# Turning x by VectorE blocks and a trip through memory in the last stage, with the experts one piece of heads later

## The reference, cut to what matters

```python
x = x + attention(layernorm(x))     # 32 heads of 128, ends in y @ Wo.T  (512 <- 4096)
n = layernorm(x)
result = n @ W.T + b
q, k   = n @ Wq.T, n @ Wk.T          # 8 experts of 32 each
w      = softmax(sum(q * k, -1) / sqrt(32))      # one weight per expert
h      = n @ A.T                     # 8 experts of rank 16
x = x + result + einsum(w, h, Bm)
```

## Time and profile before

| | us |
|---|---|
| median of 3 runs | 1765.15 (1765.02 to 1765.41) |
| the profiled execution | 1765.26 |
| its span in the trace | 1763.4 |
| TensorE busy | 1738.6 (99%) |
| VectorE busy | 1271.4 (72%) |
| ScalarE busy | 715.1 (41%) |
| GpSimd busy | 851.6 (48%) |

### The profile page before, as it was taken

The page is one execution under the profiler, slowest core; times in us unless marked ns, Lnnn a source line. Parts: engine busy times, 40 slices in busy tenths (PEclk is TensorE's granted clock), DMA queues, the critical chain, the costliest instruction groups (busy, mean ns, idle before and its releaser), DMA issues. The chain is left out here.

```text
span 1763.4 us, 27984 instructions
## 1 busy us (share of the span) xinstructions
PE 1738.6 (99%) x8744; PEld 1468.0 (83%) x8744; DVE 1271.4 (72%) x2353; ACT 715.1 (41%) x2232; POOL 851.6 (48%) x862
## 2 busy tenths in 40 slices
PE   7999999999999999999999999999999999999998
PEld 6788888888888888888888888888778888888886
DVE  5327899998989989889999998998864333333332
ACT  3424444444455444544445444544652212121111
POOL 3126676667667666767666666766401101010101
PEclk9999999999999999999999999999999999999999
DMA  6235323433433333332433333333572323232321
GB/s 208 91 100 146 91 73 118 116 93 112 120 87 118 118 86 111 114 102 77 118 117 90 111 120 88 118 88 105 195 253 76 99 78 102 76 103 74 104 73 47
DMA packets 145985, 190.31 MB, mean 108 GB/s; under 512 B 9136, under 2 KB 79792, under 8 KB 145840
## 3 DMA queue, kind: packets, MB, share of 16 engines
q1 hardware_dynamic: 145840, 188.58, 35.6%
HBM read 141.89 MB, written 46.66 MB: 107 GB/s over the span
## 5 line engine op out<-in xcount | busy, mean ns | idle before, releaser
L117 POOL TENSOR_TENSOR q<-raw_wo_early 128x512 f32<-128x512 f32 x128 | 165.3, 1291 | 195.8 <-DVE raw_wo_early L109 195.6
L88 PE MATMUL p_proj<-shared,wq_hi 128*128 128x512 f32 x744 | 244.5, 389 | 0.0
L1135 ACT ACTIVATE square<-p_y 128x128 f32<-128x128 f32 x512 | 134.2, 277 | 220.1 <-PE p_y L849 218.7
L1877 POOL TENSOR_TENSOR var<-mv,eps 128x1 f32<-128x1 f32 x16 | 3.0, 190 | 402.6 <-DVE mv L1727 402.6
L849 PE MATMUL p_y<-v_tok,probs 128*128 128x128 f32 x1024 | 183.0, 276 | 0.0
L1007 DVE SCALAR_TENSOR_TENSOR z<-p_y,srstd,gate 128x128 f32<-128x128 f32 x512 | 143.7, 343 | 51.6 <-issue 34.5
L1110 ACT ACTIVATE probs<-g_row,stab 128x128 f32<-128x128 f32 x512 | 164.3, 407 | 24.2 <-POOL g_row L1244 24.1
L88 PE MATMUL p_kept<-wg_hi,shared 128*128 128x512 f32 x560 | 173.1, 390 | 0.0
L1258 POOL TENSOR_TENSOR xw_lo<-xw_raw,xw_hi 128x512 fp32r<-128x512 f32 x96 | 131.0, 1364 | 86.0 <-ACT xw_hi L1151 86.0
L88 PEld LDWEIGHTS p_proj<-shared,wq_hi 128*128 128x128 f32 x744 | 139.7, 188 | 30.4 <-DVE raw_wo_early L109 1.2
L1266 POOL TENSOR_TENSOR srstd<-svar,mhalf 128x4 f32<-128x4 f32 x128 | 157.7, 1232 | 10.0
(11 more groups left out here) (244 smaller groups left out, 4395.3 us busy)
## 6 DMA issues: line engine op xcount, KB each, us to landing
g_row<-g_scratch SPq DMA_DIRECT2D x128, 256.0 KB, 5.1
z_scratch<-z_st SPq DMA_DIRECT2D x256, 128.0 KB
w_raw<-z_scratch SPq DMA_DIRECT2D x62, 512.0 KB, 6.7
e_row<-e_scratch SPq DMA_DIRECT2D x96, 256.0 KB, 4.1
w_raw<-in_wq_t SPq DMA_DIRECT2D x16, 512.0 KB, 7.3
w_raw<-in_wg_t SPq DMA_DIRECT2D x16, 512.0 KB, 5.6
v_tok<-v_scratch SPq DMA_DIRECT2D x32, 256.0 KB, 2.9
v_scratch<-n_xin SPq DMA_DIRECT2D x20, 256.0 KB, 2.3
```

The costliest lines, as they stand in the source:

```text
L88: mm = pe.matmul(out, lhs[a], rhs[e], start=(i == 0 and j == 0), stop=(i == len(pairs) - 1 and j == 2))
L117: pool.tensor_tensor(out, keep["rope_a"][:, s, :], keep["rope_b"][:, s, :], ALU.add).then_inc(keep["roped"], 1)
L1135: s = act.activation(square[:, h, :], p_y[c % 2][:, h, :], ACT.Square, scale=2.0 / float(np.sqrt(D)), accum_out=ssum[:, c, h:h + 1])
```

## The change

It has two parts, both in steps 1 to 13 (`by_blocks`); tiles 0, 14 and 15 keep TensorE's transposes.

**The turn of x.** VectorE writes the normalised x into the PSUM tile `p_xt` in place of `xn`, then turns it in 32x32 blocks into `xn` (`dve.transpose`, a STREAM_TRANSPOSE of 128x512). Each block is then right in itself but stands in the wrong place. SyncE stores the four groups of 32 partitions with four DMAs of 64 KB into a new tensor in memory (`x_scratch`), in runs of 32 values, which is 128 bytes, and waits until all four have landed; one DMA of 256 KB then loads the turned x into `xt_raw`, the same bytes as `xt_lo`, in runs of 128 values, which is 512 bytes. ScalarE and VectorE make the high and low part from there and no longer from PSUM.

**The order.** TensorE runs pieces 0, 1 and 2, then the experts, piece 3, `turn_hw`, `dense` and `combine`. VectorE makes the low part of z (i+1, 1) before it waits for the inverse root, that of (i+1, 2) before `x_low`, and that of (i+1, 3) before `weigh`. ScalarE makes the high part of (i+1, 2) before `x_high`. SyncE issues the four stores after the load of (i+1, 2), then the load of (i+1, 3), then the load of the turned x, and only then the load of tile i+1's input.

The rest of the diff folds semaphores that counted for one engine alone into one, in the norm stage and in `weigh`, with the same waits.

```diff
             def step(b, u, has_next):                      # SyncE
                 if has_before(i):
                     store(b, u - 1)
                 load_z(ahead(i)[1:2])
+                if by_blocks(i):
+                    store_blocks(i)
+                    load_z(ahead(i)[2:3])
+                    load_turned(i)
                 if has_next:
                     wait_ge(sp, out_sent[1 - s], 8 * (i - s) + 16 * s)
                     load_x(b, u + 1)
-                load_z(ahead(i)[2:])
+                load_z(ahead(i)[3 if by_blocks(i) else 2:])
+
+            def store_blocks(i):
+                sp.wait_ge(x_blocks_set, i)
+                for a in range(P // BL):
+                    sp.dma_start(x_dram.rearrange("(b j) t -> j b t", j=BL)[:, :, a * BL:(a + 1) * BL],
+                                 xn[a * BL:(a + 1) * BL, :].rearrange("j (b t) -> j b t", t=BL)).then_inc(x_blocks_out, 16)
+
+            def load_turned(i):
+                sp.wait_ge(x_blocks_out, 16 * (P // BL) * i)
+                sp.wait_ge(f_done, i)
+                sp.dma_start(xt_raw[:, :, :], x_dram.rearrange("(k p) t -> p k t", p=P)).then_inc(xt_in, 16)
...
             def step(b, u, has_next):                      # TensorE
-                if has_next:
-                    wo_piece(i + 1, 1 - s, 0)
-                turn_x(i)
-                if has_next:
-                    wo_piece(i + 1, 1 - s, 1)
-                experts(i)
-                if has_next:
-                    wo_piece(i + 1, 1 - s, 2)
+                if by_blocks(i):
+                    for j in range(NP - 1):
+                        wo_piece(i + 1, 1 - s, j)
+                    experts(i)
+                    wo_piece(i + 1, 1 - s, NP - 1)
                     turn_hw(i)
-                    wo_piece(i + 1, 1 - s, 3)
                     dense(i)
...
                 dve.bn_aggr(mv[:, :], stats[:, :]).then_inc(mv_set, 1)      # VectorE
+                if by_blocks(i):
+                    z_low(*ahead(i)[0])
                 dve.wait_ge(rstd_set, i + 1)
...
+                dve.tensor_scalar(p_xt[:, :, :].rearrange("p k t -> p (k t)"), x1, mv[:, 0:1], rstd[:, 0:1],
+                                  ALU.subtract, ALU.mult).then_inc(xn_set, 1)
+                dve.wait_ge(xn_set, i + 1)
+                wait_ge(dve, x_blocks_out, 16 * (P // BL) * (i - 1))
+                dve.transpose(xn[:, :], p_xt[:, :, :].rearrange("p k t -> p (k t)")).then_inc(x_blocks_set, 1)
...
             def step(b, u, has_next):                      # ScalarE
+                if by_blocks(i):
+                    z_high(*ahead(i)[0])
+                    z_high(*ahead(i)[1])
+                    x_high(i)
+                    z_high(*ahead(i)[2])
+                    save_keys(i)
+                    exponent(i)
+                    z_high(*ahead(i)[3])
+                    save_hw(i)
+                    return
```

More of the change, by code:

```diff
@@ L178, in norm_stage @@
             "pre", "ex", "u1", "df", "rc", "ln", "log"))
-        gg_set, G_set, wexp_set, eg_set = sem("n_gg_set"), sem("n_G_set"), sem("n_wexp_set"), sem("n_eg_set")
+        G_set, wexp_set, eg_set = sem("n_G_set"), sem("n_wexp_set"), sem("n_eg_set")
         dt_set, dt_up_set, ln_dt_set, ln_dt_min = sem("n_dt_set"), sem("n_dt_up_set"), sem("n_ln_dt_set"), sem("n_ln_dt_min")
-        row_set = [sem(f"n_row_set{k}") for k in range(TAB)]
+        row_set = sem("n_row_set")
         tabs_done, tabs_saved, g_out = sem("n_tabs_done"), sem("n_tabs_saved"), sem("n_g_out")
@@ L1480, in output_stage @@
         keys, qk = (free[0][:, 0, i * E * DK:(i + 1) * E * DK].rearrange("p (e d) -> p e d", e=E) for i in range(2))
-        xt_part = [sb(f"xt_{n}", [P, KT, P], F32R) for n in ("hi", "lo")]
+        xt_raw, xt_low = twice(nc, ctx, "xt_lo", [P, KT, P])
+        xt_part = [sb("xt_hi", [P, KT, P], F32R), xt_low]
+        x_dram = keep["x_dram"]
         stats, mv, var, rstd, mhalf = sb("stats", [P, 6]), sb("mv", [P, 2]), sb("var", [P, 1]), sb("rstd", [P, 1]), sb("mh", [P, 1])
@@ L1535, in xt, with xt_whole @@
             return xt_last if is_last(i) else xt_part
+        def xt_whole(i):
+            return xt_raw[:, :, :] if by_blocks(i) else p_xt[:, :, :]
         def xt_free(engine, i):
@@ L1544, in has_before, with by_blocks, turned_by_pe @@
             return not (isinstance(i, int) and i == 0)
+        def by_blocks(i):
+            return not (isinstance(i, int) and not 0 < i < NT - 2)
+        def turned_by_pe(i):
+            return 1 if by_blocks(i) else {0: 0, NT - 2: 1, NT - 1: 2}[i]
         def has_ahead(i, by):
@@ L1683, in step @@
                 has_next = has_next and not (isinstance(i, int) and i == 0)
-                if has_next:
-                    wo_piece(i + 1, 1 - s, 0)
-                turn_x(i)
-                if has_next:
-                    wo_piece(i + 1, 1 - s, 1)
-                elif not has_before(i):
-                    heads(pe, keep, p_out[1], 1, NP - 1, 1, opening=True, some=range(AFTER, HP))
-                experts(i)
-                if has_next:
-                    wo_piece(i + 1, 1 - s, 2)
+                if by_blocks(i):
[3 more added lines that the diff above has]
+                    wo_piece(i + 1, 1 - s, NP - 1)
                     turn_hw(i)
-                    wo_piece(i + 1, 1 - s, 3)
                     dense(i)
                 else:
+                    turn_x(i)
+                    heads(pe, keep, p_out[1], 1, NP - 1, 1, opening=True, some=range(AFTER, HP))
+                    experts(i)
                     dense(i)
@@ L1734, in x_low @@
                 xt_free(dve, i)
-                dve.tensor_tensor(xt(i)[1][:, :, :], p_xt[:, :, :], xt(i)[0][:, :, :].bitcast(F32),
-                                  ALU.subtract).then_inc(xt_lo_set, 1)
+                dve.tensor_tensor(xt(i)[1][:, :, :], xt_whole(i), xt(i)[0][:, :, :].bitcast(F32), ALU.subtract).then_inc(xt_lo_set, 1)
             def weigh(i):
@@ L1742, in weigh @@
                 dve.wait_ge(prod_set, i + 1)
[L1743 to L1747, removed]
+                dve.tensor_reduce(sc[:, :], qk, AX.X, ALU.add).then_inc(max_set, 1)
+                dve.wait_ge(max_set, 3 * i + 1)
+                dve.reduce_max(mx[:, :], sc[:, :], AX.X).then_inc(max_set, 1)
+                dve.wait_ge(max_set, 3 * i + 2)
+                dve.tensor_scalar(nmx[:, :], mx[:, :], -SCALE, None, ALU.mult).then_inc(max_set, 1)
                 dve.wait_ge(ew_set, i + 1)
@@ L1766, in step @@
                 normalise(i, s)
[L1767 to L1772, removed]
-                x_low(i)
[L1774 to L1779, removed]
+                if by_blocks(i):
+                    z_low(*ahead(i)[1])
+                    x_low(i)
+                    z_low(*ahead(i)[2])
+                    weigh(i)
+                    z_low(*ahead(i)[3])
+                    add_dense(i, s)
+                    return
+                opening_low(dve, keep, len(OPENING) - KT)
+                opening_low(dve, keep, len(OPENING) - KT + 1)
+                x_low(i)
+                opening_low(dve, keep, len(OPENING) - KT + 2)
+                opening_low(dve, keep, len(OPENING) - KT + 3)
+                for ii, j in ahead(i):
                     z_low(ii, j)
                 weigh(i)
-                for ii, j in ahead(i)[2:]:
-                    z_low(ii, j)
                 add_dense(i, s)
@@ L1813, in x_high @@
             def x_high(i):
-                act.wait_ge(xt_done, i + 1)
+                if by_blocks(i):
+                    act.wait_ge(xt_in, 16 * i)
+                else:
+                    act.wait_ge(xt_done, turned_by_pe(i) + 1)
                 xt_free(act, i)
-                act.activation(xt(i)[0][:, :, :], p_xt[:, :, :], ACT.Copy).then_inc(xt_hi_set, 1)
+                act.activation(xt(i)[0][:, :, :], xt_whole(i), ACT.Copy).then_inc(xt_hi_set, 1)
             def save_keys(i):
@@ L1835, in step @@
                 i, s = TB * b + u, u % 2
-                if has_before(i):
-                    for ii, j in ahead(i)[0:1]:
-                        z_high(ii, j)
+                if by_blocks(i):
+                    z_high(*ahead(i)[0])
[6 more added lines that the diff above has]
+                    save_hw(i)
+                    return
                 x_high(i)
[L1840 to L1843, removed]
+                for ii, j in ahead(i):
                     z_high(ii, j)
```

37 lines of the change are left out of this document (19 added, 18 removed).

## The result

| | median us | ratio to before | 95% interval |
|---|---|---|---|
| before, beside it (6 runs) | 1765.79 | | |
| changed (6 runs) | 1772.88 | 1.004 | 1.0027 to 1.0052 |

The change makes the kernel 7.1 us slower; the sum of the forecast was 6.4 us. The profiled execution has a span of 1771.7 us against 1763.4.

What follows compares the result with a forecast made beforehand. TensorE, busy 383.73 of 383.73 us in steps 1 to 13, bounds the kernel. 13 x (0.94 wait - 0.45 transposes) = 6.4 us on profiled 1765.26 gives 1771.7, forecast as 1771.5, range 1763 to 1786.

Steps and rivals of the forecast that it cites:

- z is last at piece 2: Piece 2 on TensorE: z lands T+9.76 (T: first matmul of piece 0); wait 0.94 us, step 0.49 longer.
- The transposes' 0.45 us: Four transposes leave TensorE: 0.45 us a step, 5.9 in all, only lengthening the wait while z is last.
- x is there in time: Before the experts: turned x ready at T+16.0, 1.7 us before TensorE asks, so no added wait.
- A packet of 128 bytes costs 13 ns as a write: Block stores of turned x: 13 ns a packet taken from reads, 28 ns the upper end; stores take 1.7 us.
- Rival 2: Before the experts' first matmul: x late too, 13 us for each microsecond late, on top of 6.4; 20%.
- The four engines: Finished tile's store, 4 x 32 rows, uses 4 of 16 DMA engines; the z load behind it takes 8 us.
- Rival 3: TensorE's clock falls to 1.2 GHz after its wait; once a step it costs 22 us, giving 1794; 3%.

Runs made afterwards that it cites:

- e2: Changed kernel with the load of z (i+1, 2) issued ahead of the finished tile's store: 1759.28 us, 0.9960 of before.
- e1: Changed kernel with only the new order kept, x turned by TensorE's transposes, no blocks through memory: 1773.71 us, 1.0041 of before.
- e3: Changed kernel with TensorE's transposes back, the new order kept, and z (i+1, 2) loaded ahead of the store: 1765.22 us, 0.9995 of before.
- e7: Changed kernel with the finished tile's store cut into four DMAs of 32 rows, each to its right rows: 1755.43 us, 0.9945 of before.
- e4: Changed kernel with the experts back between pieces 1 and 2, so blocks without the new order: 1850.27 us, 1.0475 of before.
- e9: Kernel before the change, with only the finished tile's store cut into four DMAs: 1761.65 us, 0.9980 of before.

## Why the prediction was right, step by step

**z is last at piece 2, +0.49 us a step.** Right in mechanism and in size: the steps grew by 6.8/13 = 0.52 us. The landing was summed as T+9.76 and came at T+9.77, the effective begin was summed as T+12.25 and came there in step 7. e2 shows it by taking the wait away, e1 shows that the order brings it without any block. The estimate came from step 14, where the kernel before already ran this order once, and from one mean wait.

**The transposes' 0.45 us are won only if nothing else is last.** Right: e1 and the changed kernel differ by nothing that can be measured, e2 and e3 by 0.47 us a step.

**x is there in time, by 1.7 us.** The sum was right, its terms were not. The blocks were ready at T+6.4, 1.0 later than worked out: GpSimd's add stood behind `z_low` (0.9 us), so that the normalised x began at T+4.78 in place of T+4.15; writing it to PSUM took 0.81 in place of 0.55; and the turn began 0.13 behind it. The stores made up for it: they had landed at T+11.2, 0.5 sooner than summed from the end of the z load, and the load was issued then; it took 3.4 us, not 2.9. Errors of +1.0, -0.5 and +0.5 us, and a margin that comes out as summed. The first error was hidden because the load could start only when the stores on the late engines had landed: in e2 and e7, where those engines are free sooner, the blocks are ready at the same T+6.4 and the load goes out at T+10.0 on average, 1.2 us sooner. That the other two cancel is luck.

**A packet of 128 bytes costs 13 ns as a write.** The value taken, from loads, holds for stores. It was worked out with 84 ns for a packet of 2 KB, which none of the rows shows; the packet records of the trace before do, with a median of 84 ns for 2 KB and 13 for 128 bytes. The changed kernel while the block stores run, 1521 to 1523 us:

```profile
DMA packets 1715, 0.34 MB, mean 172 GB/s; under 512 B 1647, under 2 KB 1647, under 8 KB 1715
q1 hardware_dynamic: 1715, 0.34, 85.6%
```

85.6% of 16 engines' 2 us is 27.4 us; less 68 packets of 2 KB at 84 ns, 21.7 us over 1647 small ones: 13 ns, and 13 ns is also the median in the records of all its block stores' packets. The Trainium skill ("DMA: Bandwidth & Descriptors", "Specifications") has a DMA engine do a read-modify-write below 512 bytes; if these stores do one, their packets' time doesn't show it. Rival 2 had its place right and was not reached.

**The four engines.** Right, and now shown by e7. The rule for the number of engines stands in the Trainium skill, "DMA: Bandwidth & Descriptors", in the section "Why a DMA increments its semaphore by 16 and not by 1", and not in the one that the prediction names. The trace agrees for this store: a share of 0.25 of 16 engines is 4.

**The clock.** Rival 3 rightly had little weight for a wait under 1 us: the clock stays at 1.00 in all steps of the changed kernel. e4 shows it for waits of 4.4 to 5.3 us, and dearer than rival 3 had it: 25 us in place of 22, as more than half of the steps have the low clock for twice as long.

**What was not in the sum:** the 1.2 us of span before step 1. They are not the change's. 1.1 of them stand already where TensorE begins the output stage after a pause, at 1292.93 in the changed kernel and at 1291.81 before; e9, whose kernel is that of before up to this point, begins it at 1292.59, and the ten profiles other than that of before have it between 1292.41 and 1293.35. So the profile of before is the odd one, and its execution, 1765.26 us, was 0.5 below the median of the six runs. Its pauses differ as well: 2.26 us up to 1278.12 and 1.87 before the output stage, where the other ten have 1.4 and 3.6 to 4.0. What makes them fall one way or the other stays open.

## What to carry to other kernels

Where the engine that bounds the kernel never waits, work taken off it is won only down to the next input: list for each of its steps when each input is ready, and the smallest margin behind the change tells more than the time of what is removed. Moving work away from between two consumers spends the margin of the second; look at who loads its data, and how late. And when a DMA lands late, look at how many engines the one ahead of it uses: its shape, not its bytes, held the queue here, and splitting it is what made the change pay: 3.7 us in the kernel before, and 9.9 together with the change, which alone lost 7.1.

## What the runs showed of the hardware beyond that

- With a last store of 4 x 32 rows of 2 KB the span ends 6.3 us after the last add, with the same bytes as four DMAs of 32 rows 3.5 us after it; a 512 KB load issued behind such stores lands after 7.8 against 3.9 us.
- GpSimd's add of a 128x1 tile takes 0.19 us alone and 1.12 beside a VectorE op with two SBUF inputs, ending with it; its add of 128x512 takes 2.20 us with such an op beside it and 1.29 without. By the Trainium skill ("SBUF — State Buffer", "Who interferes with whom"), a `tensor_tensor` with both inputs in SBUF contends with GpSimd's reads and the one that comes second is held until the first ends; the trace agrees.
- After each of e4's 13 waits of 4.4 to 5.3 us TensorE ran at 1.2 GHz (granted clock 0.50), which lasted about 3.4 us in six steps and about 6.8 in seven. The pause of 3.6 to 4.0 us before the output stage was followed by a granted clock of 0.50 to 0.58 in the ten profiles that have it, the pause of 2.26 us of before by 0.52 and 0.63. After pauses of 1.87 and 1.4 us, and after the 13 waits under 1 us of the changed kernel, the clock stayed at 1.00.
